# Indirect transfers of an attention and expert layer: GpSimd's scatters and gathers spaced by waits, and its row arithmetic moved

## What is computed

```python
x = x + attn(layernorm(x))                 # window 32, per sequence
h = layernorm(x)
logits = h @ router_w.T                    # 8 experts
weights, selected = sparsemixer_eval(logits, 0.01)   # two experts per token
for e in range(8):
    y = silu(h @ w_gate[e].T) * (h @ w_up[e].T)
    out = out + dense_w[:, e:e+1] * (y @ w_down[e].T)
x = x + out
```

## Time and profile before

| what | us |
|---|---|
| timed runs | 561.99, 562.23, 567.3 |
| median of the timed runs | 562.23 |
| span of the profiled execution, first to last instruction | 673.3 |
| its busy time: PE, DVE, ACT, POOL | 550.8, 424.6, 370.5, 345.8 |
| scatters, 128 instructions | 126.9 |
| gathers, 128 instructions | 122.3 |

### The profile page before, as it was taken

How to read it: one execution, slowest core, us unless ns; L and a number is a source line. 1 busy time by engine, 2 the same in 40 slices (tenths; PEclk the granted TensorE clock), 3 DMA queues, 4 the chain that set the end, 5 groups by cost and what they waited for, 6 DMA issues and landing times.

```text
span 673.3 us, 23426 instructions
## 1 busy us (share of the span) xinstructions
PE 550.8 (82%) x7519; PEld 473.6 (70%) x7519; DVE 424.6 (63%) x1700; ACT 370.5 (55%) x1170; POOL 345.8 (51%) x536
## 2 busy tenths in 40 slices
PE   3899999999999999987657669888887878887860
PEld 1578887777878777875537569777787778776850
DVE  5788898898989988883554226355444454544452
ACT  4467776666757766651246437455554555554530
POOL 3333346667776666763343381435455444556355
PEclk9999999999999999995756779899899899999895
DMA  7333333233332222222111223334444443443333
GB/s 215 67 72 74 71 81 96 65 82 82 69 72 46 53 45 53 53 48 62 33 54 44 65 67 96 99 114 135 115 120 126 111 123 102 126 122 107 103 107 82
DMA packets 126310, 58.20 MB, mean 86 GB/s; under 512 B 54000, under 2 KB 121712, under 8 KB 126192
## 3 DMA queue, kind: packets, MB, share of 16 engines
q1 hardware_dynamic: 117424, 39.03, 23.3%
q0 software_dynamic: 8192, 16.79, 8.6%
q10 hardware_dynamic: 576, 0.88, 0.4%
HBM read 28.15 MB, written 24.58 MB: 78 GB/s over the span
## 4 chain that ended last, share of the span: by engine, by line
PE 69%; another core or an unknown queue 9%; issue 8%; ACT 5%; DMA 3%; DVE 2%; POOL 2%; SPq 1%; ACTq 1%; POOLq 0%; DVEq 0%
PE chb L727 16%; PE pv L581 7%; PE chb L639 6%; PE pm L592 5%; PE pp L752 5%; PE pp L661 5%; PE pv L752 4%; PE chb L630 4%; PE chb L626 3%; PE tp L744 2%; PE tp L684 2%; POOL ga L1368 2%; PE tp L554 2%; PE tp L560 2%
## 5 line engine op out<-in xcount | busy, mean ns | idle before, releaser
L1368 POOL DMA_INDIRECT ga<-expert_out,row_all x128 | 122.3, 955 | 137.1 <-DVE yb L1257 83.9
L1297 POOL DMA_INDIRECT expert_in<-xn,slot_r x128 | 126.9, 992 | 121.5 <-DVE slot_r L921 96.5
L727 PE MATMUL chb<-xbT,wcur 128*128 128x128 f32 x1144 | 162.4, 288 | 0.0
L727 PEld LDWEIGHTS chb<-xbT,wcur 128*128 128x128 f32 x1144 | 150.6, 205 | 0.0
L1250 DVE TENSOR_TENSOR hT<-sil,chb 128x256 f32<-128x256 f32 x143 | 60.1, 420 | 114.2 <-ACT sil L507 86.3
L507 ACT ACTIVATE sil<-chb 128x256 f32<-128x256 f32 x143 | 54.9, 384 | 124.2 <-PE chb L727 57.2
L417 ACT ACTIVATE pT<-chb 128x512 f32<-128x512 f32 x128 | 77.1, 602 | 69.8 <-PE chb L639 59.5
L938 DVE TENSOR_REDUCE mx<-chb 128x8 f32<-128x512 f32 x128 | 86.7, 685 | 18.0 <-PE chb L639 13.9
L524 ACT COPY wcur<-wgu 128x512 f32 x143 | 89.9, 629 | 5.6 <-issue 5.3
L744 PE MATMUL tp<-ident,xb 128*128 128x128 f32 x143 | 42.5, 297 | 48.9 <-issue 38.6
L581 PEld LDWEIGHTS pv<-vext,pT 128*64 128x64 f32 x1984 | 68.1, 140 | 13.8 <-issue 13.3
(11 more groups left out here) (140 smaller groups left out, 1051.1 us busy)
## 6 DMA issues: line engine op xcount, KB each, us to landing
xb<-expert_in SPq DMA_DIRECT2D x143, 64.0 KB
expert_out<-yb SPq DMA_DIRECT2D x71, 128.0 KB
xa<-x SPq DMA_DIRECT2D x16, 256.0 KB
out<-oo SPq DMA_DIRECT2D x31, 128.0 KB
qk<-qk SPq DMA_DIRECT2D x64, 48.0 KB
wgu<-w_gu SPq DMA_DIRECT2D x16, 128.0 KB
expert_in<-xn,slot_r POOLq DMA_INDIRECT x128
ga<-expert_out,row_all POOLq DMA_INDIRECT x128
```

The source lines that it names most:

```text
L727: last = nc.tensor.matmul(chb[:, b % 4, n * P:(n + 1) * P], wcur[:, b % 3, n * P:(n + 1) * P], xbT[:, b % 4, :], start=True, stop=True)
L1297: nc.gpsimd.indirect_dma_start(xs_dram, bass.IndirectOffsetOnAxis(ap=slot_r[:, q % 4, 2 * v + k:2 * v + k + 1], axis=0), xn2[:, t % 16, :] ...
L1368: nc.gpsimd.indirect_dma_start(ga[:, q % 2 * TPS + v, j, :], None, ys_dram[0:min(blocks, LIVE) * P, :], bass.IndirectOffsetOnAxis(ap=row_a ...
```

## The change

Three things in GpSimd's program. `rows(0)` comes after step 78 (the scatters of group 12), ahead of the scatters of groups 13 and 14 (steps 79 to 86); group 15's eight scatters are issued one by one after the first eight pairs of gathers. A scatter of tile 44 or later waits until the scatter before it has landed (`one_landed`). A pair of gathers of tiles 1 to 55 waits until the pair before it has landed. The gathers stand now in a generator, `fetch`.

```diff
--- before.py
+++ after.py
@@ -58,6 +58,7 @@
 C_FIRST = 5
 MEM = 8
 S_MOE = NT + L_PV
+ROWS_STEP, FETCH_STEP = L_SCAT + (SPLIT + 1) * TPS, L_SCAT + (SEQS - 1) * TPS
 QUICK = 6
 L_LATE = 80
 W_STEP, PIECES = 10, 3 * EXP
@@ -1292,8 +1293,14 @@
                 nc.gpsimd.memset(vext[g * WIN:(g + 1) * WIN, :, :, KF + g], 1.0).then_inc(c_mem, 1)
             nc.gpsimd.memset(qk[0:WIN, :, 2 * P:3 * P], 0.0).then_inc(c_mem, 1)
 
+            def one_landed(n):
+
+                pool.wait_ge(scat[n // (2 * TPS) % 4], (n // (8 * TPS) * 2 * TPS + n % (2 * TPS) + 1) * 16)
+
             def scatter(t, k):
                 q, v = t // TPS, t % TPS
+                if t + L_SCAT - L_RMS >= NT:
+                    one_landed(2 * t + k - 1)
                 nc.gpsimd.indirect_dma_start(
                     xs_dram, bass.IndirectOffsetOnAxis(ap=slot_r[:, q % 4, 2 * v + k:2 * v + k + 1], axis=0),
                     xn2[:, t % 16, :], None).then_inc(scat[q % 4], 16)
@@ -1333,7 +1340,7 @@
                     scatter(out_t, 1)
 
             pool.wait_ge(c_mem, MEM)
-            for s in range(STEPS):
+            for s in range(ROWS_STEP):
                 step(s)
 
             link = run(pool, row_chain)
@@ -1354,21 +1361,38 @@
                 link(nc.gpsimd.tensor_copy(row_all[:, q0 * TPS:q1 * TPS, :].rearrange("p (q v) k -> p q (v k)", q=q1 - q0),
                                            part_slots))
 
+            rows(0)
+            def fetch(q, part):
+
+                blocks = 2 * TPS * (q + 1) + (part + 1) * (SLACK + 1)
+                for n in range(U // 2):
+                    pool.wait_ge(yb_out[n], blocks // U * 16)
+                wait(pool, comb_ok, (q - 1) * TPS)
+                for v in range(TPS):
+                    k = q * TPS + v
+                    if q < SEQS - 2 and (v or part == 0):
+                        pool.wait_ge(yb_ok, 2 * TPS * (q + 1) + 2 * (SLACK + 1) + 2 * v + 1)
+                    if 0 < k < (SEQS - 2) * TPS:
+                        pool.wait_ge(gath[(k - 1) % (2 * TPS)], ((k - 1) // (2 * TPS) + 1) * 32)
+                    for j in range(2):
+                        nc.gpsimd.indirect_dma_start(
+                            ga[:, q % 2 * TPS + v, j, :], None, ys_dram[0:min(blocks, LIVE) * P, :],
+                            bass.IndirectOffsetOnAxis(ap=row_all[:, q * TPS + v, j:j + 1], axis=0))\
+                          .then_inc(gath[q % 2 * TPS + v], 16)
+                    yield
+
+            for s in range(ROWS_STEP, FETCH_STEP):
+                step(s)
+            late = (n for n in range(2 * (FETCH_STEP - L_SCAT), 2 * NT))
             for part, (q0, q1) in enumerate(PARTS):
-                rows(part)
+                if part:
+                    rows(part)
                 for q in range(q0, q1):
-                    blocks = 2 * TPS * (q + 1) + (part + 1) * (SLACK + 1)
-                    for n in range(U // 2):
-                        pool.wait_ge(yb_out[n], blocks // U * 16)
-                    wait(pool, comb_ok, (q - 1) * TPS)
-                    for v in range(TPS):
-                        if q < SEQS - 2 and (v or part == 0):
-                            pool.wait_ge(yb_ok, 2 * TPS * (q + 1) + 2 * (SLACK + 1) + 2 * v + 1)
-                        for j in range(2):
-                            nc.gpsimd.indirect_dma_start(
-                                ga[:, q % 2 * TPS + v, j, :], None, ys_dram[0:min(blocks, LIVE) * P, :],
-                                bass.IndirectOffsetOnAxis(ap=row_all[:, q * TPS + v, j:j + 1], axis=0))\
-                              .then_inc(gath[q % 2 * TPS + v], 16)
+                    for _ in fetch(q, part):
+                        n = next(late, None)
+                        if n is not None:
+                            pool.wait_ge(slot_ok, n // (2 * TPS) + 1)
+                            scatter(n // 2, n % 2)
 
     return nc
```

## The result

The kernel after takes 687.14 us (686.86 to 691.65, 4 runs), the kernel before 563.11; the ratio is 1.221, with an interval of 1.216 to 1.226. The change makes it slower by 124 us. Slower was forecast, 35 us of it, with an upper end of 622 us: the direction and the mechanism hold, the size does not.

What follows compares the result with a forecast made beforehand. TensorE was taken to bound the kernel before; after the change GpSimd's chain would end last: 75.8 + 8.3 + 203.3 + 4.6 + 24.1 = 316 us, ending at 596, about 598 with stores and boundaries; range 557 to 622.

Steps and rivals of the forecast that it cites:

- The sum: Kernel before, undisturbed durations of attention steps, 150 slots and the end: 542.5 us, against 562 timed, so almost no pauses.
- the drained steps: Fourteen steps drained between the first slots: 1.4 us each assumed, for the 20 us lacking to 562.
- GpSimd's chain: GpSimd's scatters, rows and gathers from group 11's slots to the end: ends last, 576 to 622 us, chance 0.56.
- what would show it: Signs in the profile after; if right, the span grows less than the timed run, or not at all.
- Rows ahead: Part 0's rows moved before groups 13 to 15: no cost to GpSimd, contention nothing, 8.3 us at most.
- Group 11's scatters: Serial scatters ahead of SyncE's first block load: without pauses, delay of 0 to 1 us.
- rival with relief of the queues: Spaced transfers remove pauses in the MoE slots: gain of 10 to 15 us, 549 us, chance 0.19.
- a term of the sum: One summand of GpSimd's chain from group 11's slots: scatters, rows, 56 pairs, last gathers; 316 us, ending at 596.
- (d): Gathers of tiles 1 to 55: a pair waiting for the pair before takes 3.93 us against 2.52; from below 3.28.
- (e): Sum of GpSimd's chain to the end: 342.5 us with row durations, 288 by lower bounds, 316 as taken.
- the durations of the rows: Full profile durations, scatter 2.67 and pair 3.93 us, in GpSimd's chain: 342.5 us, ending at 622.
- the ten slots of lead: Gathers issued ahead of VectorE's combinations: 14.5 us, 10.8 after landing, gone after eleven pairs at 1.0 us lost each.

Runs made afterwards that it cites:

- e1: The kernel before once more, no edit, with its own profile: 563.99 us, ratio 1.0022, profiled span 563.8.
- e2: The kernel before, with only the wait of each pair of gathers for the pair before added: 661.76 us, ratio 1.1762.
- e4: The kernel after, but a pair of gathers waits for the pair two before it: 575.55 us, ratio 1.0278.
- e10: The kernel after, with the second gather of a pair also waiting for the first to land: 774.38 us, ratio 1.3735.
- e5: The kernel before, with only the rows of part 0 moved ahead of the scatters of groups 13 to 15: 564.07 us, ratio 0.9998.
- e8: The kernel after, without the scatters' waits; rows ahead, group 15 between the pairs and pair waits as after: 672.34 us, ratio 1.1911.
- e6: The kernel before, with only the scatters from tile 44 on issued one at a time: 592.71 us, ratio 1.0518.
- e9: The kernel after without pair waits or scatter waits, leaving only the new order: 568.13 us, ratio 1.0061.
- e7: The kernel after, with a pair's two waits swapped, predecessor's landing first, then the block's copy: 668.50 us, ratio 1.1865.

## Why the prediction was right in kind and short by 89 us

What held, point by point:

- The timed run has next to no pauses. The sum reached 542.5 us from rows and laid the other 20 on the drained steps without a row for them; e1 bears the choice out (slots of 1.45 us, span 563.8).
- Slower, because a pair takes longer than two slots, and then GpSimd's chain ends last (e2, e4, e10).
- The span grew by 12 us (673.3 to 685.6) where the timed run grew by 124, as "what would show it" has it.
- Rows ahead cost nothing (e5). Group 11's scatters do not hold up the first block: the first block's copy is at 323.3 us in e1, at 326.3 in after, and at 327.4 in e8, which is after without the scatters' waits.
- No rival with relief of the queues: with spaced transfers nothing got faster (e5, e6, e9).

What failed is a term of the sum, the price of a pair in (d), "1.26 + 2.40 + 0.27 = 3.93 us", and with it the step behind it in (e), "I take the landing 0.3 us shorter ... pair 3.63". The measured mean is 4.77. Of the gap of 1.14 us to the value I used:

- 0.43 is the restart. I took 0.27 us from a gather released by VectorE's copy. Behind a landing that is waited for by an instruction of its own it is 0.70 (the chain of after), and e7 turned it off in three pairs of four, worth 18.6 us.
- 0.4 to 0.5 is the landing. I started from 2.40 of the tail, and went below it. In the middle of the MoE part it is 2.5 to 2.6. I had taken the quiet row and then a discount that no row gave; full and quiet stretches should have been the two ends.
- the rest, 0.2 to 0.3, are single long landings, 2.9 to 4.3 us, twelve of the 55 that end a pair, each beside a packet of an instruction queue (the section on the result).

55 x 1.14 = 63 us. The scatters give the next piece: from 285.50 to 387.21, less 9.1 for the rows and the gap behind them, 32 scatters took 2.9 us each and not 2.37, 17 us; the chain began 5 us later than I had it. 63 + 17 + 5 = 85 of the 89 us. The other four are at the end: from the start of pair 55 to the last instruction it is 31.6 us, and the sum had 3.63 + 24.1 = 27.7. The upper bound of 622 was made with "the durations of the rows" as if they were the worst; the sum had no room for a landing later than the one row that I had, nor for a restart longer than 0.27, and that is why the result lies outside the range.

One step of (d) did not come about as told: the ten slots of lead were to be used up after eleven pairs. In after the first gather (387.21) comes later than the first combination of e1 (380.8), so the lead was gone before the first pair, and that combination, at 391.1, already waits. The sum follows GpSimd's chain and does not hang on it.

For the landing the Trainium skill (DMA: Bandwidth & Descriptors, section "Anatomy of one DMA — SWDGE (gpsimd) path") has a fixed 2.0 us and bytes over a rate, an estimate of 2.15 us here. The scatters of e6, mostly at 2.2 to 2.4 us from start to landing, are near it; the gathers of after, at 2.4 to 4.3, are not. No run here shows what the fixed part is made of. That a landing is paid once for each wait, and disappears behind another transfer in flight, is shown by e10 and e4.

## What to carry to other kernels

A wait for one's own last transfer turns a queue into a chain: price one link as issue plus landing plus restart, and compare it with the period of the loop that needs the data. What it is longer by, times the count, is the loss: here 4.77 less 2.9 us, times 55, is 103 us, and e2 lost 100. Take the landing from the busiest stretch, not from the tail, and keep one more transfer in flight before asking for anything else; e4 did that with one wait fewer. Where a profiled execution stands far from the timed runs, add up the undisturbed durations: if the sum gives the timed run, the slack seen in the profile isn't there; here the sum left 20 of 562 us to an assumption, and only a second profile (e1) settled it.

## What was not expected of the hardware

The order of two waits ahead of an indirect transfer is worth 0.5 us each time: 0.70 us from landing to start when the landing is awaited by an instruction of its own, about 0.25 when the transfer instruction itself waits (e6, e7). A spread of landings of one and the same kind of gather from 2.4 to 4.3 us within one run, with an instruction packet beside each long one. And one execution of the kernel before, profiled, that was 111 us longer than the median, with pauses over several engines at once; in the 57 timed runs of before that stand beside the experiments it did not come back (560.0 to 572.2 us).
